# A Mamba-style mixer block and a talking-heads attention block on one core: softplus and Newton steps of block 0 moved from GpSimd to VectorE and ScalarE, and TensorE's order of layers changed

## The reference, cut to what matters

```python
xc    = silu(conv4(x @ W_in.T) + conv_b);  res = x @ W_res.T
delta = softplus(xc @ W_dt.T + b_dt)                 # [L, 128]
for t: h = exp(delta_t * A) * h + delta_t * Bp * xc_t # 16 states per feature
       y_t = sum_n h[:, n] * Cp[:, n]
x = layernorm(x + ((y + xc * Dp) * silu(res)) @ W_out.T)     # norm "na"
h = silu(x @ w1) * (x @ w2)                          # 128 -> 512
h = gelu(h @ h1);  h = gelu(h @ h2)                  # 512 -> 512, twice
x = layernorm(x + h @ w3)                            # norm "nb"
```

## Time and profile before

| | us |
|---|---|
| median of 3 runs (5043.0 to 5049.14) | 5045.71 |
| the profiled execution | 5042.12 |
| its span, first to last instruction | 5040.8 |
| PE busy | 4159.0 (83%) |
| DVE busy | 4359.3 (86%) |
| ACT busy | 2733.9 (54%) |
| POOL busy | 1117.8 (22%) |

### The profile page before, as it was taken

One profiled execution on the slowest core, in us unless ns is written; L12 is line 12 of the kernel. 1 busy time (PEld: TensorE's weight loads), 2 busy tenths in 40 slices (PEclk: granted clock), 3 DMA queues, 4 the chain that ended last, 5 costly groups with the idle time before them and its releaser, 6 DMA issues.

```text
span 5040.8 us, 77383 instructions
## 1 busy us (share of the span) xinstructions
PE 4159.0 (83%) x20627; PEld 2891.3 (57%) x20627; DVE 4359.3 (86%) x19673; ACT 2733.9 (54%) x7261; POOL 1117.8 (22%) x3450
## 2 busy tenths in 40 slices
PE   4888888856888888888888888888888888888886
PEld 3677777743555555555555555555555555555554
DVE  6777777716999999999999999999999999999995
ACT  4555555534555555555555555555555555555553
POOL 2333333321212121212121111212212121211210
PEclk8999999976999999999999999999899998999987
DMA  2000000001111111111111111111111111111110
GB/s 86 8 9 10 10 9 9 6 11 20 25 25 26 21 21 21 21 21 22 21 21 21 21 21 24 23 21 21 26 25 26 21 21 21 21 21 21 21 20 3
DMA packets 163304, 103.67 MB, mean 21 GB/s; under 512 B 73584, under 2 KB 160688, under 8 KB 162224
## 3 DMA queue, kind: packets, MB, share of 16 engines
q1 hardware_dynamic: 162864, 98.71, 9.3%
HBM read 18.97 MB, written 8.39 MB: 5 GB/s over the span
## 4 chain that ended last, share of the span: by engine, by line
DVE 45%; PE 30%; issue 10%; ACT 10%; SPq 2%; DMA 2%; POOL 1%; DVEq 0%; POOLq 0%; ACTq 0%
DVE W L1335 16%; DVE top L1339 12%; PE bank L209 6%; PE bank L362 5%; DVE y L659 4%; PE bank L951 3%; ACT SN L1162 3%; DVE T L1346 3%; PE bank L1023 2%; PE bank L973 2%; PE bank L175 2%; SPq L859 2%; DVE top L1360 2%; DVE hs L649 2%; DMA T<-SN 2%
## 5 line engine op out<-in xcount | busy, mean ns | idle before, releaser
L1339 DVE MAX8 top<-W 128x8 f32<-128x252 f32 (+11 forms) x4704 | 1385.7, 333 | 3.3
L1335 DVE MATCH_REPLACE8 W<-top,W 128x252 f32<-128x252 f32 (+13 forms) x3936 | 1276.8, 331 | 0.0
L963 PE MATMUL bank<-T,pre 128*128 128x12 f32 (+31 forms) x2048 | 544.6, 350 | 279.4 <-ACT T L1168 158.8
L963 PEld LDWEIGHTS bank<-T,pre 128*128 128x128 f32 x2048 | 359.8, 208 | 617.0 <-ACT T L1168 274.9
L1480 POOL TENSOR_SCALAR posts<-post,share 128x128 f32<-128x128 f32 x1024 | 362.6, 372 | 1154.8 <-DVE share L1311 1154.8
L649 DVE TENSOR_TENSOR_SCAN hs<-dA,dx 128x256 f32<-128x256 f32 x512 | 391.9, 766 | 210.0 <-issue 207.2
L1168 ACT ACTIVATE T<-bank 128x12 f32<-128x12 f32 (+31 forms) x1024 | 288.9, 282 | 519.9 <-PE bank L963 518.4
L973 PE MATMUL bank<-posts,T 128*128 128x128 f32 (+7 forms) x2048 | 463.6, 315 | 64.9 <-POOL posts L1480 63.3
L1496 POOL TENSOR_TENSOR T<-T,w_mask 128x8 f32<-128x8 f32 x1024 | 186.4, 203 | 1460.5 <-ACT T L1168 1460.5
L1162 ACT ACTIVATE SN<-bank,rq 128x260 f32<-128x260 f32 (+1 forms) x1024 | 365.5, 430 | 192.0 <-PE bank L951 172.5
L973 PEld LDWEIGHTS bank<-posts,T 128*128 128x128 f32 (+7 forms) x2048 | 301.0, 185 | 195.0 <-POOL posts L1480 124.9
(11 more groups left out here) (228 smaller groups left out, 8506.6 us busy)
## 6 DMA issues: line engine op xcount, KB each, us to landing
T<-SN SPq DMA_DIRECT2D x32, 130.0 KB
x_in<-in_xT SPq DMA_DIRECT2D x32, 128.0 KB, 2.2
x_mid<-x_b SPq DMA_DIRECT2D x32, 128.0 KB, 1.7
xb<-x_mid SPq DMA_DIRECT2D x32, 128.0 KB, 2.1
out_y<-x_d SPq DMA_DIRECT2D x32, 128.0 KB, 3.3
T<-SN SPq DMA_DIRECT2D x32, 126.0 KB
T<-SN SPq DMA_DIRECT2D x32, 122.0 KB
T<-SN SPq DMA_DIRECT2D x32, 118.0 KB
```

Of the source, the lines that this page charges most:

```text
L963: pe.matmul(MIX[:, 0:seen_by(g)], pre[:], scores(b, g), start=True, stop=True).then_inc(premixed, 1)
L1335: dve.match_replace(work, best, src, MASKED).then_inc(ranked, 1)
L1339: dve.max(best, work).then_inc(ranked, 1)
```

## The change

GpSimd does nothing in block 0's periods any more. What it did is spread: y begun (as an ACT Copy with scale Dp) and rl (as Relu) go to ScalarE; u, err and the difference go to VectorE as three instructions; the norm takes the variance straight from PSUM with epsilon as ScalarE's bias, ScalarE adds a square of the guess, and VectorE does the Newton step in two instructions and folds the rest into the finish. The diff, without the removed class members that stand again in another form:

```diff
-    def dve_lift(self, dve, k):
-        dve.wait_ge(self.varied, k + 1)
-        dve.tensor_scalar(self.var[:], self.bank[:, SEQ:2 * SEQ], LN_EPS, None, ALU.add).then_inc(self.lifted, 1)
-
     def act_log(self, act, k):
-        act.wait_ge(self.lifted, k + 1)
-        act.activation(self.t[:], self.var[:], ACT.Ln).then_inc(self.root.logged, 1)
+        act.wait_ge(self.varied, k + 1)
+        if k:
+            act.wait_ge(self.root.stepped, Root.STEPS * k)
+        act.activation(self.t[:], self.bank[:, SEQ:2 * SEQ], ACT.Ln, bias=self.eps[:]).then_inc(self.root.logged, 1)
...
-    def pool_root(self, pool, k):
-        self.root.pool_step(pool, k, self.var[:], self.rs[:], self.t[:])
+    def act_guess2(self, act, k):
+        act.wait_ge(self.root.guessed, k + 1)
+        act.activation(self.rs2[:], self.rs[:], ACT.Square).then_inc(self.lifted, 1)
+
+    def dve_miss(self, dve, k):
+        dve.wait_ge(self.lifted, k + 1)
+        dve.scalar_tensor_tensor(out=self.t[:], in0=self.bank[:, SEQ:2 * SEQ], scalar=LN_EPS, in1=self.rs2[:], op0=ALU.add,
+                                 op1=ALU.mult).then_inc(self.root.stepped, Root.STEPS - 1)
+
+    def dve_step(self, dve, k):
+
+        dve.wait_ge(self.root.stepped, Root.STEPS * k + Root.STEPS - 1)
+        dve.scalar_tensor_tensor(out=self.t[:], in0=self.t[:], scalar=3.0, in1=self.rs[:], op0=ALU.subtract,
+                                 op1=ALU.mult).then_inc(self.root.stepped, 1)
 
     def dve_finish(self, dve, k, result):
         dve.wait_ge(self.root.stepped, Root.STEPS * (k + 1))
-        dve.tensor_tensor(result, self.bank[:, 0:SEQ], self.rs[:], ALU.mult).then_inc(self.normed, 1)
+        dve.scalar_tensor_tensor(out=result, in0=self.bank[:, 0:SEQ], scalar=-0.5, in1=self.t[:], op0=ALU.mult,
+                                 op1=ALU.mult).then_inc(self.normed, 1)
...
-    ABS, LOG_B, SQUARE_A, LOG_SP, LOG_A = 2, 5, 8, 8, 12
-    Z, LIFT_B, RL, GATE, END_B, LIFT_A, DELTA, END_A = 1, 0, 3, 6, 11, 8, 10, 14
-    VAR_B, DT, OUT_A = 0, 1, 3
+    ABS, BEGIN, LOG_B, SQUARE_A, LOG_SP, LOG_A = 2, 4, 5, 6, 8, 9
+    Z, PLUS, MISS_B, GATE, MISS_A, DELTA = 1, 4, 8, 5, 11, 10
+    VAR_B, DT, W2, OUT_A, VAR_A = 0, 0, 2, 3, 0
...
             if seq(n):
                 pe.wait_ge(na.normed, n + 1)
                 f0.pe_w1(pe, n, 0, x_a[n % 3][:])
+                f0.pe_w1(pe, n, 1, x_a[n % 3][:])
             if seq(l):
...
-            if seq(n):
-                f0.pe_w1(pe, n, 1, x_a[n % 3][:])
             for k in range(HC):
...
+                if k == W2 and seq(n):
+                    f0.pe_w2(pe, n, 0, x_a[n % 3][:])
+                    f0.pe_w2(pe, n, 1, x_a[n % 3][:])
                 if k == OUT_A and seq(o):
...
-            if seq(n):
-                f0.pe_w2(pe, n, 0, x_a[n % 3][:])
-                f0.pe_w2(pe, n, 1, x_a[n % 3][:])
-            if seq(o):
-                na.pe_var(pe, o)
             for k in range(HC):
+                if k == VAR_A and seq(o):
+                    na.pe_var(pe, o)
                 if seq(n):
                     f0.pe_h1(pe, n, k)
...
+                    act.activation(rl[:], FBANK[:, 0:SEQ], ACT.Relu, bias=b_dt).then_inc(rectified, 1)
...
+                if s == BEGIN and seq(f):
+                    act.wait_ge(xc_made, f + 1)
+                    if f >= 2:
+                        act.wait_ge(z_made, f - 1)
+                    act.activation(y[f % 2][:], xc[f % 2][:], ACT.Copy, scale=Dp).then_inc(y_begun, 1)
...
-                    dve.tensor_scalar(rl[:], FBANK[:, 0:SEQ], b_dt, 0.0, ALU.add, ALU.max).then_inc(rectified, 1)
+                if t == PLUS and seq(f):
...
+                    dve.tensor_scalar(u[:], e_[:], 1.0, None, ALU.add).then_inc(plus_made, 1)
+                if t == PLUS + 1 and seq(f):
+                    dve.wait_ge(plus_made, f + 1)
+                    dve.scalar_tensor_tensor(out=err[:], in0=u[:], scalar=1.0, in1=e_[:], op0=ALU.subtract,
+                                             op1=ALU.subtract).then_inc(erred, 1)
+                if t == PLUS + 2 and seq(f):
...
+                    dve.tensor_tensor(err[:], rl[:], err[:], ALU.subtract).then_inc(parted, 1)
...
-        for p in range(PERIODS):
-            f, o, l = p, p - 2, p - 5
-            if seq(f):
-                if f >= 2:
-                    pool.wait_ge(z_made, f - 1)
-                pool.wait_ge(xc_made, f + 1)
-                pool.tensor_scalar(y[f % 2][:], xc[f % 2][:], Dp, 1.0, ALU.mult, ALU.mult).then_inc(y_begun, 1)
...
-            if seq(l):
-                nb.pool_root(pool, l)
-            if seq(o):
-                na.pool_root(pool, o)
```

More of the change, by code:

```diff
@@ L255, with __init__ @@
 class WideNorm:
-    def __init__(self, room, sems, name, bank, meanmat):
-        self.bank, self.meanmat = bank, meanmat
-        self.sq, self.var, self.rs, self.t = (room.sb(f"{name}_{n}", [P, SEQ]) for n in ("sq", "var", "rs", "t"))
+    def __init__(self, room, sems, name, bank, meanmat, eps):
+        self.bank, self.meanmat, self.eps = bank, meanmat, eps
+        self.sq, self.rs, self.rs2, self.t = (room.sb(f"{name}_{n}", [P, SEQ]) for n in ("sq", "rs", "rs2", "t"))
         self.centred = sems.sem(name + "_centred")
@@ L457, in mixer_phase @@
     x_a, x_b = room.sbs("x_a", [P, SEQ], 3), room.sbs("x_b", [P, SEQ], 2)
-    na = sh.na = WideNorm(room, sems, "na", bank[1], sh.meanmat)
-    nb = sh.nb = WideNorm(room, sems, "nb", bank[2], sh.meanmat)
+    eps = room.sb("eps", [P, 1])
+    na = sh.na = WideNorm(room, sems, "na", bank[1], sh.meanmat, eps)
+    nb = sh.nb = WideNorm(room, sems, "nb", bank[2], sh.meanmat, eps)
     x_loaded = sems.sems("x_loaded", NX)
-    padded, tapped, folded, conv_ready = (sems.sem(n) for n in ("padded", "tapped", "folded", "conv_ready"))
+    eps_set, padded, tapped, folded, conv_ready = (sems.sem(n) for n in ("eps_set", "padded", "tapped", "folded", "conv_ready"))
     out_folded, out_ready, w3_folded, w3_ready = (sems.sem(n) for n in ("out_folded", "out_ready", "w3_folded", "w3_ready"))
@@ L563, in scalar @@
         act.wait_ge(const_made, 1)
+        act.wait_ge(eps_set, 1)
         def decay(b, s):
@@ L606, in scalar @@
                     nb.act_guess(act, l)
+                if s == LOG_B + 2 and seq(l):
+                    nb.act_guess2(act, l)
                 if s == SQUARE_A and seq(o):
@@ L615, in scalar @@
                     na.act_guess(act, o)
+                if s == LOG_A + 2 and seq(o):
+                    na.act_guess2(act, o)
             act.preload_act_table_set(GELU)
@@ L676, in vector @@
                     dve.tensor_tensor(z[:], y[o % 2][:], sres[o % 3][:], ALU.mult).then_inc(z_made, 1)
[L677 to L680, removed]
+                if t == PLUS and seq(f):
+                    dve.wait_ge(exped, f + 1)
                     if f:
-                        dve.wait_ge(delta_made, f)
-                    dve.tensor_scalar(rl[:], FBANK[:, 0:SEQ], b_dt, 0.0, ALU.add, ALU.max).then_inc(rectified, 1)
+                        dve.wait_ge(logged, f)
+                    dve.tensor_scalar(u[:], e_[:], 1.0, None, ALU.add).then_inc(plus_made, 1)
[4 more added lines that the diff above has]
+                if t == PLUS + 2 and seq(f):
+                    dve.wait_ge(erred, f + 1)
+                    dve.wait_ge(rectified, f + 1)
+                    dve.tensor_tensor(err[:], rl[:], err[:], ALU.subtract).then_inc(parted, 1)
+                if t == MISS_B and seq(l):
+                    nb.dve_miss(dve, l)
+                if t == MISS_B + 1 and seq(l):
+                    nb.dve_step(dve, l)
                 if t == GATE and seq(n):
@@ L687, in vector @@
                     f0.dve_gate(dve, n, 1)
-                if t == END_B and seq(l):
+                if t == MISS_B + 2 and seq(l):
                     if l >= 2:
@@ L691, in vector @@
                     nb.dve_finish(dve, l, x_b[l % 2][:])
-                if t == LIFT_A and seq(o):
-                    na.dve_lift(dve, o)
+                if t == MISS_A and seq(o):
+                    na.dve_miss(dve, o)
+                if t == MISS_A + 1 and seq(o):
+                    na.dve_step(dve, o)
                 if t == DELTA and seq(f):
@@ L698, in vector @@
                         dve.wait_ge(decayed, STATES * (f - 1))
-                    dve.tensor_tensor(delta[f % 2][:], rl[:], lu[:], ALU.add).then_inc(delta_made, 1)
+                    dve.tensor_tensor(delta[f % 2][:], err[:], lu[:], ALU.add).then_inc(delta_made, 1)
                 if t == DELTA + 1 and seq(f):
@@ L705, in vector @@
                     dve.tensor_tensor(dx[f % 2][:], delta[f % 2][:], xc[f % 2][:], ALU.mult).then_inc(dx_made, 1)
-                if t == END_A and seq(o):
+                if t == MISS_A + 2 and seq(o):
                     if o >= 3:
@@ L716, in gpsimd @@
         last.then_inc(padded, 1)
+        pool.memset(eps[:], LN_EPS).then_inc(eps_set, 1)
         pool.wait_ge(sh.weights0_in, WEIGHTS0)
         f0.pool_scale(pool)
```

11 lines of the change are left out of this document (3 added, 8 removed).

## The result

The changed kernel takes 4878.02 us in the median (4875.54 to 4880.61, 4 runs) against 5047.43 us (5043.0 to 5051.09, 4 runs) for the kernel before on the same chip: ratio 0.9665, 95% interval 0.9648 to 0.9682, 169 us less. 4880 was forecast. The profiled execution has a span of 4876.0 us. A further run of the kernel before was made beside the changed kernel's, so its median here is 1.7 us above the 5045.71 of the first three.

A forecast was written before the change was run, and what follows sets the result against it. A loop through ScalarE, VectorE and TensorE was taken to bound block 0. Savings of 139 us in filled periods, 15 in filling, 2 at the first delta and 8 in emptying, together 164, gave 4880 us; range 4840 to 4930.

The forecast's parts named there:

- The loop: Block 0's turn from decays through scans, gate 1, h1, conv, w1 and silu: 25.2 us a period instead of 30.56.
- w1 ahead of w3: TensorE in block 0: w1's second half moved up starts decays at C+6.50 instead of 8.43, gain 1.93 us.
- GpSimd: VectorE in block 0: all 3.9 us a period of work slowed beside GpSimd goes; bounds 0 and 3.9.
- New VectorE work: Seven added VectorE instructions for three removed in block 0, at 0.33 to 0.38 us each, bounds 0.2 and 0.47.
- The stall: ScalarE waits 4.2 us at the square of na for the output product; VectorE loses 1.0 us of it.
- The clock: TensorE's granted clock in block 0: expected at 1.00, with two gaps of 0.6 us left per turn.
- Filling: Start of block 0's pipeline: five intervals of some 16, 19, 23, 23, 25 us instead of 121.0, saving 15.
- the first (the clock): Rival: TensorE's clock still falls in most block 0 periods, costing 32 x 1.0 us, 4912 us; 15%.
- the third (GpSimd): Rival: slow VectorE scans weren't GpSimd's doing, 2.9 us a period stay, 4971 us; 7%.
- The second: Rival: square's stall matters less or short VectorE instructions are cheaper; TensorE bounds at 24.6 us, total 4860 us; 12%.
- The fourth: Rival, slower: TensorE runs from conv's start to the output product at 1.2 GHz, 218 us lost, 5096 us; 3%.
- The fifth: Rival, slower: four more VectorE instructions simply count, 1.5 us in each of 32 periods, 5091 us; 2%.

The follow-up runs named there:

- w1 and w_dt: Kernel before with w1's second half ahead of w3 and w_dt one block of h2 earlier on TensorE: 4986.97 us, ratio 0.9883.
- move-alone kernel: Changed kernel with TensorE's order as before; only GpSimd's work moved, with the new places on VectorE and ScalarE: 4929.64 us, ratio 0.9771.

## Why the prediction was right

The profile after and the experiments bear out the mechanism nearly step by step. The total is nearer than its terms were, and that part is luck; see the sum below.

- *The loop.* Forecast 25.2 us a period, measured 25.02. Forecast positions from the start of conv against measured (C = 502.93): with x_a's lateness of 0.6 us added, w1's first half at C+2.8 against 2.60, the decays at C+7.1 against 7.07 (510.00), the square of na at C+17.2 against 17.15, h1 at C+18.2 against 18.12, the next conv at C+25.2 against 25.03.
- *w1 ahead of w3.* The gain of 1.93 us was right as a shift of the decays, and in the full change only half of it arrives (31 us of 62); both were in the working, since scan 7 was held by the square. That part of the shift would be lost on the kernel before, where w_dt and the variance of nb had not moved, was not seen.
- *GpSimd.* 3.9 us of slowed work a period were taken as gone, and the scans are at 0.68 to 0.70. With GpSimd back on unrelated tiles VectorE has 3.6 us more of it and the time is 4976, where the rival's sum had 4971. The narrow reading of the Trainium skill, "Advanced Engine Details and Errata", section "VectorE Performance Modes", fails: instructions with two tensors in SBUF were slowed to more than double in the rows of the kernel with GpSimd at work again.
- *New VectorE work.* 0.33 to 0.38 us each was right: miss and step start 0.33 us ahead of the next instruction, u 0.20 (515.83 to 516.03, a duration of 0.28), below the price taken, within its bounds.
- *The stall.* 4.2 us of ScalarE at the square were forecast, 1.0 of them passed on to VectorE; measured 3.97 and 0.96. TensorE's wait for the square was forecast at 0.64: by the starts (519.45 and 0.43, then 520.52) it is 0.64, of which the trace shows 0.47 as idle. w1 starts 0.44 us late, of which 0.28 is shown as idle, where 0.63 was forecast.
- *The clock* was forecast at 1.00 in block 0. It is 1.00 in the filled stretch and 0.72 while the pipeline fills (0.69 in the kernel before), a stage of which the prediction read no clock.
- *The sum.* The terms were off by more than the total. Filled periods: 139 forecast, 143.9 measured (25.02 us for 25.2). Filling: 15 forecast, 10.3 measured; the turns there are 17.3, 17.9, 24.2, 25.7 and 25.6 us where 16, 19, 23, 23 and 25 were taken. Full-clock prices had been used for a stage in which TensorE has 0.72. The largest miss, the fourth turn, shows it: h1 at its start took 9.76 us (clock 0.74 from 95 to 106 us). In the kernel with the output product ahead of w2 the same h1 took 7.15 us (clock 1.00 from 100 to 108 us), and the same turn 23.07 us. First the changed kernel's h1, then that kernel's:

```profile
95.51 9.76 PE L374 MATMUL bank<-f_a,w_f0h 128*128 128x256 f32 x32 [4.57 <-DVE f_a L370]
```

```profile
100.57 7.15 PE L374 MATMUL bank<-f_a,w_f0h 128*128 128x256 f32 x32 [1.05 <-DVE f_a L370]
```

- *The rest of the sum.* The first delta: 2 forecast, 5.7 measured, but 4.0 of it is the weights' landing (VectorE's first instruction starts at 17.25 instead of 21.26 us), which is no part of the change; 1.7 remain. Emptying: 8 forecast, 8.8 measured. Block 1 was to stay as it was and took 3.8 us more. That need not be an effect of the change: the stretch behind block 0's last norm differs by up to 7 us between the traces of these kernels, whose block 1 is the same (3983.4 to 3990.2 us). So +4.9, -4.7, +3.7, +0.8 and -3.8 us nearly cancel, and that 164 stood against 164.8 is luck; that the turn was within 1% is not.

Of the rivals, the first (the clock) and the third (GpSimd) were shown wrong for the change by its own profile, and the experiments show both mechanisms to be real where their conditions hold. The second, TensorE bounding at 24.6 us a turn and 4860 us, is not the changed kernel's state (25.02), but it is that of the kernel with the square of na behind decay 8 (24.48 us, 4861). The fourth, a stretch of each turn at 1.2 GHz, is ruled out by the clock of 1.00 in the filled stretch. The fifth took VectorE for the bound, as the busiest engine. That is so over the whole kernel and was not so in block 0: from 200 to 780 us of the kernel before TensorE is busy for 493 us and VectorE for 446. VectorE got more work there and the kernel is faster, since neither share was the bound; the loop was, as the earlier trace rows had it.

## What to carry to other kernels

In a hand-ordered pipeline over several engines, write the loop that sets the period as positions in time from one anchor, with prices from start to start; what one part shifts is not what the kernel gains (1.9 us a period for the second half of w1 were worth 1.4 on the kernel before and 0.9 on the changed one, and TensorE's whole order 52 us where w1 alone seemed to hold 62). Work put on GpSimd isn't free for VectorE even where nobody waits for it, so an offload has to earn more than it slows. Before an instruction with a late input is moved up, count what is queued behind it, and move its producer up first.

## What the runs showed of the hardware

GpSimd at work made many of VectorE's instructions slower: with two SBUF tensors up to 2.2 times in the mean (err 421 to 945 ns), and the one-tensor u 2.8 times (288 to 810 ns). Two kinds with one tensor in PSUM, miss of nb (418 and 411 ns) and the gates (686 and 678 ns), were not. Matmuls that do nothing, put into a wait of TensorE, made the kernel 29 us faster, since the granted clock no longer fell from 2.4 to 1.2 GHz behind it. Waits of 3.5 to 3.8 us each period went with a granted clock of 0.94, one of 3.1 us (w1 and w_dt) with 0.96. The length of one wait doesn't settle it: one of 1.6 us in the move-alone kernel left the clock at 1.00, while the kernel with GpSimd at work again has 1.4 us at the gates, up to 1.4 more for x_a, and 0.98. The stretch in which the pipeline fills has 0.72.
